# One gather issued between two writes: SyncE's queue in a fused AdaLN and FFN kernel

## The reference

```
x = x + L0_ffn(L0_cond(x, cond))      # mix of 32 channels per batch, then gated LoRA (4 experts, top 2)
x = x + L1_ffn(L1_cond(x, cond, b))   # grouped conv of 9 taps over 512 positions, then a 512x512
                                      # product plus gated LoRA (8 experts, top 2)
# L1_cond:
out = conv_general_dilated(x, weight, padding=[(4, 4)], feature_group_count=4)   # 32 -> 32 channels
out = out + (c @ c_weight.T)[:, :, None] + bias[None, :, None]
# L1_ffn:
main = xf @ weight.T
out = main + lora        # lora: x @ lora_A[e], weighted by the router, @ lora_B[e]
```

## Time and profile before

| | |
|---|---|
| median of 3 runs | 316.49 us (316.31 to 319.11) |
| the profiled execution, its own time | 317.21 us |
| its span in the trace | 315.4 us |
| TensorE busy | 294.3 us, 93% |
| VectorE, ACT, GpSimd busy | 63%, 40%, 31% |
| granted TensorE clock | full all through |
| bytes moved | 52.76 MB, mean 167 GB/s |

### The profile page before, as it was taken

The page is one execution under the profiler, slowest core; times in us unless marked ns, Lnnn a source line. Parts: engine busy times, 40 slices in busy tenths (PEclk is TensorE's granted clock), DMA queues, the critical chain, the costliest instruction groups (busy, mean ns, idle before and its releaser), DMA issues.

```text
span 315.4 us, 6197 instructions
## 1 busy us (share of the span) xinstructions
PE 294.3 (93%) x2015; PEld 242.6 (77%) x2015; DVE 198.1 (63%) x503; ACT 124.7 (40%) x261; POOL 97.5 (31%) x127
## 2 busy tenths in 40 slices
PE   7999989989998999999989999999999899898994
PEld 6999867658886888778867887788777777686882
DVE  1369764633749464946493749474958455878785
ACT  4424535423822382238223822382227326112330
POOL 5345215114211421142114121412112226216660
PEclk9999999999999999999999999999999999999999
DMA  5968399694299439943984299429644980004887
GB/s 133 282 100 270 120 243 220 184 203 100 108 281 177 104 120 267 181 100 121 277 166 103 84 289 190 99 94 241 129 101 153 222 158 0 0 2 150 326 326 268
DMA packets 74024, 52.76 MB, mean 167 GB/s; under 512 B 44156, under 2 KB 61004, under 8 KB 74000
## 3 DMA queue, kind: packets, MB, share of 16 engines
q1 hardware_dynamic: 72752, 51.75, 64.9%
q10 hardware_dynamic: 848, 0.55, 0.7%
q0 software_dynamic: 400, 0.16, 0.3%
HBM read 35.67 MB, written 16.78 MB: 166 GB/s over the span
## 4 chain that ended last, share of the span: by engine, by line
PE 62%; DMA 14%; DVE 10%; ACT 5%; issue 4%; SPq 2%; POOL 0%; DVEq 0%; ACTq 0%; POOLq 0%
DMA xg<-x1d 12%; PE ps_g L1093 10%; PE ps_d L1093 9%; PE ps_a L1054 8%; PE ps_c L1228 7%; PE ps_a L1043 4%; PE ps_t L1244 3%; DMA x1d<-xq 2%; PE ps_d L1269 2%; ACT xq L602 2%; ACT xT L553 2%; PE ps_d L1114 2%; PE ps_d L1270 2%; PE ps_v L1066 1%; PE ps_d L1436 1%
## 5 line engine op out<-in xcount | busy, mean ns | idle before, releaser
L489 POOL TENSOR_TENSOR o1l<-o,o1h 128x512 fp32r<-128x512 f32 x30 | 39.3, 1311 | 156.8 <-ACT o L614 156.8
L1093 PE MATMUL ps_d<-wt_hi,o1h 128*128 128x336 f32 (+1 forms) x120 | 41.1, 342 | 0.3 <-DVE y_all L929 0.3
L1228 PE MATMUL ps_c<-xg,cw 96*32 96x512 f32 x256 | 34.1, 605 | 5.4 <-DMA xg<-x1d 5.4
L1093 PE MATMUL ps_d<-wt_hi,o1l 128*128 128x336 f32 (+1 forms) x120 | 38.7, 323 | 0.0
L1093 PE MATMUL ps_d<-wt_lo,o1h 128*128 128x336 f32 (+1 forms) x120 | 38.6, 322 | 0.0
L923 DVE TENSOR_TENSOR oT<-ps_c,biasT 128x512 f32<-128x512 f32 x32 | 21.9, 685 | 24.3 <-PE ps_c L1228 24.3
L602 ACT ACTIVATE xq<-y_all 128x512 f32 (+1 forms) x29 | 32.2, 1138 | 11.5 <-DVE y_all L929 7.9
L1093 PE MATMUL ps_g<-wt_hi,o1h 128*128 128x336 f32 x112 | 35.6, 318 | 0.5 <-ACT tmp_all L629 0.4
L1093 PE MATMUL ps_g<-wt_hi,o1l 128*128 128x336 f32 x112 | 35.5, 317 | 0.0
L1093 PE MATMUL ps_g<-wt_lo,o1h 128*128 128x336 f32 x112 | 35.3, 315 | 0.0
L1054 PEld LDWEIGHTS ps_a<-pm,xT 128*128 128x128 f32 x256 | 29.7, 192 | 0.6 <-ACT xT L553 0.5
(11 more groups left out here) (244 smaller groups left out, 591.8 us busy)
## 6 DMA issues: line engine op xcount, KB each, us to landing
xg<-x1d SPq DMA_DIRECT2D x64, 254.0 KB, 4.6
xg<-x1d SPq DMA_DIRECT2D x32, 256.0 KB, 3.4
x1d<-xq SPq DMA_DIRECT2D x30, 256.0 KB, 2.1
xs<-in_x_dram SPq DMA_DIRECT2D x6, 1024.0 KB, 8.3
out_dram<-xT SPq DMA_DIRECT2D x16, 256.0 KB, 2.1
out_dram<-xg SPq DMA_DIRECT2D x16, 256.0 KB, 2.5
y_all<-in_x_dram SPq DMA_DIRECT2D x1, 1024.0 KB, 7.7
y_all<-in_L_ffn_weight_dram SPq DMA_DIRECT2D x1, 1024.0 KB, 6.9
```

The costliest lines, as they stand in the source:

```text
L489: pool.tensor_tensor(lo, o1[t % 2][:, :, :], hi.bitcast(fp32), ALU.subtract).then_inc(s_o1l, 1)
L1093: last = T.matmul(bank[:, 0:columns], a[:, Q - 1 - q, :], w[:, q, first:first + columns], start=(q == 0 and n == 0), stop=(q == Q - 1 and ...
L1228: last = T.matmul(ps_c[C * g:C * g + C, :], cw[0:KC, g, :, :].rearrange("p q o -> p (q o)"), xg[0:KC, t % 2, :, g, :], start=True, stop=True)
```

## The change

In every step but step 0, SyncE issues gather(s,0) behind write(s,1) instead of behind write(s,3). Before it stands a new wait until write(s,0) has landed. That was implied before: write(s,2) needs a tile that ACT reorders only after it. The wait for conv(0,2) in step 1 stays ahead of the gather and so now stands ahead of writes 2 and 3. The wait for both of these writes stays where it is.

```diff
                 else:
-                    for t in range(NT):
-                        write(s, t)
+                    write(s, 0)
+                    write(s, 1)
                     if at_step(s, 1):
                         sp.wait_ge(s_cp, 3)
-
+                    wait(sp, s_x1w[0], (s + 1) * 16)
                     gather(s, 0)
+                    write(s, 2)
+                    write(s, 3)
                     wait(sp, s_x1w[2], (s + 1) * 32)
```

## The result

| | before | after |
|---|---|---|
| median, beside each other | 317.62 us (4 runs) | 313.57 us (4 runs) |
| the profiled execution, its own time | 317.21 us | 313.72 us |
| its span | 315.4 us | 312.0 us |

The ratio of after to before is 0.9873, 95% interval 0.983 to 0.9915. Two later series of the same kernel gave 0.9851 (0.9804 to 0.9898) and 0.9831 (0.9777 to 0.9885). The change makes the kernel faster by 1.3 to 1.7%.

A forecast was written before the change was run, and what follows sets the result against it. TensorE, busy 93% of the span, was taken as the bound, so only its waits for gathers could be won. Steps 1, 2, 4 and 7 gave 1.5 + 0.43 + 1.03 + 0.84 = 3.8 us: 316.49 to 312.7, range 311.2 to 315.6.

The forecast's parts named there:

- Where the gather goes: SyncE's queue, step 4: gather issued once write 0 has landed, some 3.7 us earlier, with SyncE free before the last two writes.
- Writes land behind the gather: Writes 2 and 3, now behind the gather's packets, land later than it, by 0.6 us for each write.
- Step 1: The wait of 2.02 us before conv(1,0) goes, a new one of 0.5 comes before conv(1,1); gain 1.5 us.
- a wait of 1 us or more at a conv(s,1): Sign that the prediction is wrong, if seen before the matmuls of tile 1 in any of steps 1 to 7.
- Step 7: The wait before conv(7,0) goes and gather(7,1) is in time; gain 0.84 us.
- Steps 2 and 4: In the loop, xs load and gather(s,1) run earlier; waits at conv(2,1) and conv(4,1) shrink; gains 0.43 and 1.03 us.
- The rival that gave the loop no gain: Queue lags in steps 2 and 4 whatever is ahead; only steps 1 and 7 gain, 2.3 us, 314.2; chance 0.24.
- The slower one: Late wait for writes 2 and 3 holds xs load and gather(s,1); loss 3.2 us, 319.7; chance 0.06.
- No gain: TensorE's waits all turn into waits for VectorE or gather(s,1); 316 to 316.5 us; chance 0.11.
- all 5.06: Writes land early in step 1 and VectorE's chain follows, so all conv waits are won; 311.4 us; chance 0.07.

The follow-up runs named there:

- step 1 alone: Kernel before with the gather moved in step 1 only, steps 2 to 7 in the old order; ratio 0.9907 to the kernel before.
- steps 1 and 7 alone: Kernel before with the gather moved in steps 1 and 7, old order in steps 2 to 6; 313.18 us, ratio 0.9855.
- step 7 alone: Kernel before with the gather moved in step 7 only; ratio 0.9939 to the kernel before.
- the later load: Kernel before with the 1 MB xs load of steps 2 to 5 issued behind gather(s,1) instead of ahead of it; ratio 1.0075.

## Why the prediction was right, and where it was not

**Where the gather goes.** Right. In step 4 the gather's first DMA left at 143.49, 2.1 us behind write 0 (predicted 2.2), and its third landed in 4.7 us. SyncE was free before the next write.

**Writes land behind the gather.** Right: 4.6 and 4.8 us instead of 2.0 and 2.1. The prediction had 0.6 us for each write behind the gather; the gather's third DMA of step 1 landed at 61.5, the writes at 62.0 and 62.8, which is 0.5 and 0.8. The wait ended at 62.79, where 62.7 was worked out.

**Step 1.** The mechanism was right, the size smaller. Gather(1,1) started at 62.79 (predicted 62.8), but its third DMA left 1.3 us later instead of 1.0, since the second took 0.88 us to issue, and it landed at 68.6 instead of 68.2. TensorE was ready for conv(1,1) at 67.5, 0.2 earlier than predicted. So the new wait was 1.12 instead of 0.5, and the step gained 0.92 instead of 1.5 in this pair of profiles. The prediction had named a wait of 1 us or more at a conv(s,1) as a sign that it was wrong. By that sign the term of step 1 failed: the sum took 1.0 us for issuing a gather's three DMAs and had nothing for an issue that is itself held up. But the first profile's wait of 2.02 was the smallest of the five at this place with the old order (2.37, 2.43, 2.53 and 2.57 in the others). With the change the new wait was 0.81 to 1.39 in five profiles, and 1.90 in the one with step 1 alone. So over several executions the trade is worth about 2.4 - 1.25 = 1.1 us, and the clock comes on top.

**Step 7.** Right: 0.90 against 0.84 in the pair, and gather(7,1) was in time. In six profiles with the old order there, conv(7,0) waited 0.70 to 0.84 in four and 1.95 and 2.32 in two; with the new order it never waited.

**Steps 2 and 4.** Right in the pair (0.68 and 1.14 against 0.43 and 1.03; conv(s,0) to conv(s,2) took 11.40 and 11.54, where 11.65 was expected), and yet this is the term that was mis-sized most. The sum took the waits of one execution for the kernel's. In the four other profiles with the old order in steps 2 to 5 and without a change of the load or of the wait, they were 0.47 at conv(2,1) in one, 0.93 and 0.60 at conv(3,1) in two, and none in the fourth; and the changed kernel and the one with steps 1 and 7 alone take the same time within what six executions can tell. From conv(2,0) to conv(6,0) the profiles give 0.2 to 0.5 us, where the sum had 1.46. The reading behind the term was also in part wrong: the 11.06 us of gather(4,1)'s third DMA were put down to gather(4,0) and the load ahead of it, but with the same order it took 7.7 and 7.9 us in the profiles of step 1 alone and of step 7 alone, and 7.7 in after. What made it 11.06 in one execution isn't shown. The rival that gave the loop no gain and forecast 2.3 us was nearer for the loop, by another mechanism, and missed the rest.

**What the sum lacked.** The clock. In the profile of before it was full throughout, and the prediction had no term for it. In the 50 executions of the kernel before that the later comparisons rest on, the mean clock was 0.9925 and the mean time 317.4; in 16 of the changed kernel they were 0.9974 and 313.4. A line through the 50 falls by 2.8 us for each 0.01 of clock, so the 0.0049 are worth about 1.4 us of the 4.0, an estimate. The rest, 2.6, is the waits: 1.1 in step 1, 0.2 to 0.5 in the loop and, with a mean wait of 1.24 at conv(7,0) in the six profiles, 1.2 in step 7. That the 3.8 us of the sum came out nearly right for the median is luck: the clock's 1.4 was missing and step 7 was 0.4 too small, while the loop was about 1.1 too large and step 1 0.4. For the profiled execution 313.4 was worked out and 313.72 measured; there the four terms were off by 0.6, 0.25, 0.1 and 0.1.

**The rivals.** The slower one fails on its own deciding point: gather(1,1)'s third DMA took 4.5 us, where 5.9 was the limit. "No gain" fails on the measured 4 us, and "all 5.06" on its condition, since the writes landed late.

## What to carry to other kernels

When a transfer that the main engine waits for stands behind others in a queue that don't need to precede it, move it ahead, and in the same edit move every wait that counted on the old order: here the wait for the overtaken writes was worth another 1.8 us, of which 1.0 can be placed. A wait in one profile is one execution's; before it goes into a sum, see in a second execution whether it is there, above all a wait that hangs on a queue with several transfers in it. And a wait of TensorE can cost a stretch at half clock behind it on top of its own length: here five waits of 1.95 to 2.57 us did, and two of 2.02 and 2.32 didn't.

## What the runs showed of the hardware that was not expected

Two things here go with fetches of instructions, which the DMA view lists as packets of queues of their own.

**A write that meets a fetch.** In the profile of step 1 alone write(7,1) took 3.2 us to land instead of 2.1. The DMA view of that profile, window 235 to 238, with the two writes of tiles 1 and 2 in it, shows one packet of the instruction queue, and the line of the writes their times to landing:

```profile
q1 hardware_dynamic: 283, 0.52, 46.9%
q8 instruction: 1, 0.02, 1.9%
```

```profile
DMA to landing us min/median/max: 2.0/2.6/3.2
```

ACT's reorder of tile 3 needs that write's buffer, waited 0.95 us for it, and conv(7,0) then waited 1.95:

```profile
238.90 1.18 ACT L612 ACTIVATE xq<-y_all 128x512 f32<-128x512 f32 x1 [0.95 <-DMA x1d<-xq]
```

In the profile of before the window 237 to 240, with the writes of tiles 0 and 1, has no such packet, and both landed in 2.0 to 2.1 us:

```profile
q1 hardware_dynamic: 200, 0.38, 33.2%
```

The profile with the later load had the same meeting in step 7: one such packet in the window 237 to 240, a write that took 3.6 us, and the wait of 2.32. The profile of after had it too, in the window 235 to 238: write(7,1) took 3.4 us, but the gather of that step no longer stands behind write 3, and conv(7,0) didn't wait. Over all fourteen profiles it is the same: in the nine in which a 16 KB packet of the instruction queue starts while write(7,1) is under way, that write took 3.2 to 3.7 us, and in the five without one 2.04 to 2.06. With the old order in step 7 the two waits near 2 us are those of the two profiles with the meeting.

**An issue that waits for a fetch.** In the six profiles with the new order in step 1 and the wait for s_x1w[2] ahead of gather(1,1), the second DMA of that gather took 0.88 to 1.49 us to issue, where the first took 0.34 and the third 0.49. In all six such a packet was under way (61.50 to 62.84 in the profile of step 1 alone, 62.60 to 63.65 in that of after), and the issue ended 0.39 to 0.41 us after it. This is the 0.3 us by which the third DMA left late in step 1, and 0.6 more in the profile of step 1 alone.

The time of the fetch differs by some us between executions of nearly the same program, and no run here shows what sets it. I didn't try to move a fetch, so the coincidence is seen in every profile, and the cause is argued rather than shown.
